# A four-layer graph network on one core: the stages between the edge passes reworked, dense loops four tiles a bank at depth 128

## What is computed

```
layer 0: x = layernorm(x + sum over edges into a node of gathered, weighted rows)
layer 1: two-head attention with 5 edge attributes; the softmax runs over the edges
         of a source node; x = layernorm(x + mean of heads + bias)
layer 2: h = layernorm(x)*g+b; two-head attention (query of the destination node,
         key and value of the source node and 32 edge attributes), softmax over the
         edges into a node; res = x + out@Wp + bp;
         x = layernorm(x + res + gelu(layernorm(res)@W1 + b1)@W2 + b2)
layer 3: spline convolution: each edge weighs 8 matrices by 3 attributes; mean over
         edges, + x@root, batch norm over nodes, ELU, + x, layernorm
```

## Time and profile before

| | us |
|---|---|
| median of three runs (range) | 11246.22 (11240.04 to 11255.09) |
| the profiled execution, time | 11246.92 |
| the profiled execution, span of the trace | 11245.1 |
| VectorE busy | 7124.9 (63%) |
| GpSimd busy | 6918.7 (62%) |
| ScalarE busy | 4592.4 (41%) |
| TensorE busy | 3078.5 (27%) |

### The profile page before, as it was taken

One profiled execution on the slowest core, in us unless ns is written; L12 is line 12 of the kernel. 1 busy time (PEld: TensorE's weight loads), 2 busy tenths in 40 slices (PEclk: granted clock), 3 DMA queues, 4 the chain that ended last, 5 costly groups with the idle time before them and its releaser, 6 DMA issues. The chain is left out here.

```text
span 11245.1 us, 92785 instructions
## 1 busy us (share of the span) xinstructions
PE 3078.5 (27%) x20703; PEld 2546.4 (23%) x20703; DVE 7124.9 (63%) x9873; ACT 4592.4 (41%) x5918; POOL 6918.7 (62%) x6628
## 2 busy tenths in 40 slices
PE   1111366573000000000004566666664720000000
PEld 1111366563000000000003355555553310000000
DVE  6767788886311222118995488888885357777775
ACT  0111255452011111116772377777773234444441
POOL 6777787664577777770002577777773057777774
PEclk9999977776555555555555577777775555555555
DMA  3232322221333332224551344444441067777773
GB/s 98 78 75 89 86 64 68 70 70 51 50 111 107 111 111 103 102 100 184 200 206 43 92 136 130 128 135 129 129 135 52 23 200 235 235 235 235 235 234 90
DMA packets 722526, 1395.98 MB, mean 124 GB/s; under 512 B 409267, under 2 KB 439162, under 8 KB 714834
## 3 DMA queue, kind: packets, MB, share of 16 engines
q0 software_dynamic: 287136, 587.26, 19.4%
q1 hardware_dynamic: 406318, 636.04, 17.1%
q10 hardware_dynamic: 28996, 171.86, 4.1%
HBM read 827.48 MB, written 602.51 MB: 127 GB/s over the span
## 5 line engine op out<-in xcount | busy, mean ns | idle before, releaser
L740 POOL DMA_INDIRECT l_rows<-in_x,l_idx x1568 | 1954.3, 1246 | 669.1 <-issue 490.7
L2180 POOL DMA_INDIRECT l_rows<-table,l_idx x1568 | 1499.5, 956 | 926.9 <-issue 472.6
L1719 POOL DMA_INDIRECT l_rows<-h,l_idx x1568 | 1564.6, 998 | 614.3 <-issue 475.9
L1123 POOL DMA_INDIRECT rows<-l_rows,l_idx x1568 | 1522.6, 971 | 537.0 <-issue 497.0
L1748 PE MATMUL l_made<-l_kv_w,l_rows_t 97*128 97x256 f32 x3136 | 1139.6, 522 | 781.5 <-ACT l_kv L1778 472.4
L2255 ACT ACTIVATE l_lifted<-l_rows,l_up 128x256 f32<-128x256 f32 x1568 | 639.6, 460 | 1041.6 <-DMA l_rows<-table,l_idx 1041.6
L1748 PEld LDWEIGHTS l_made<-l_kv_w,l_rows_t 97*128 97x128 f32 x3136 | 784.2, 267 | 996.4 <-issue 852.5
L1511 PE MATMUL l_wide<-l_diag,l_ones 128*128 128x384 f32 x4 | 3.3, 928 | 3144.9 <-DVEq L1538 3144.9
L1113 DVE TENSOR_TENSOR l_rows<-l_run,l_weights_ps 128x56 f32<-128x56 f32 x56 | 12.0, 215 | 1340.9 <-POOLq L88 1340.7
L1080 ACT COPY l_rows<-l_run 128x1792 f32<-128x1792 f32 x56 | 190.7, 3405 | 1578.5 <-POOLq L88 1569.6
L826 ACT COPY l_out<-l_run 128x1792 f32<-128x1792 f32 x56 | 190.4, 3401 | 1339.5 <-DVE l_run L776 1339.5
(11 more groups left out here) (366 smaller groups left out, 12787.7 us busy)
## 6 DMA issues: line engine op xcount, KB each, us to landing
sums<-l1s_out ACTq DMA_DIRECT2D x56, 1988.0 KB, 6.6
sums<-l_out SPq DMA_DIRECT2D x112, 924.0 KB, 4.5
spread<-zeros SPq DMA_DIRECT2D x28, 3612.0 KB, 12.9
l_spread<-spread SPq DMA_DIRECT2D x112, 903.0 KB
l1s_rows<-rows SPq DMA_DIRECT2D x56, 1008.0 KB, 5.7
spread<-zeros SPq DMA_DIRECT2D x56, 938.0 KB
l_spread<-spread SPq DMA_DIRECT2D x56, 938.0 KB, 4.6
sums<-l_out ACTq DMA_DIRECT2D x56, 896.0 KB, 3.7
```

Of the source, the lines that this page charges most:

```text
L740: pool.indirect_dma_start(rows[:, b, t], None, a["x"], bass.IndirectOffsetOnAxis(ap=idx[:, b, t:t + 1], axis=0)) \
L1123: pool.indirect_dma_start(g["rows1_d"], bass.IndirectOffsetOnAxis(ap=idx[:, b, t:t + 1], axis=0), rows[:, b, t], None).then_inc(sent[b], 16)
L1719: pool.indirect_dma_start(rows[:, c.r, t, 0:C], None, g["h2_d"], bass.IndirectOffsetOnAxis(ap=idx[:, c.r, t:t + 1], axis=0)).then_inc(got[ ...
L2180: pool.indirect_dma_start(rows[:, b, t], None, g["table3_d"], bass.IndirectOffsetOnAxis(ap=idx[:, b, t:t + 1], axis=0)) \
```

## The change

Four kinds of edit, all in the stages between passes.

1. **Halves.** The 49 tiles are worked in two parts (24 and 25). In `collect_sums` and `collect_softmax` each part has its own semaphore for its gathers, so VectorE works on the first while GpSimd issues the second. TensorE's corrections get four banks (six in the softmax, three tiles a bank), and the softmax's small operations are replaced by one product for a bank and one sum for a batch of banks; scaling to the mean moved in as well. `normalise` became a class with parts and the squares on ScalarE; where a dense loop follows a gain and shift, it can start after the first part. The output is stored in parts.
2. **Steps moved.** Layer 1's attention weights are made in the program's first block; its copy of `x` is ScalarE's; loads of the output weights, their bias row and the memsets of the pass's tiles stand beside the table scatters; the memsets of the second pass's tiles stand at the end of the pass before. The head gathers are issued before the last 25 scatters (layer 1) or the last one (layer 2). Layer 2's pass loads no longer wait for the set-up of the tiles, and layer 3's pass loads indices before keys and attributes. The product with `root` runs beside the last gathers (class `RootProduct`).
3. **Dense loops.** Layer 1's end takes two tiles (`PAIRS`) a bank and runs through `Pipeline`; layer 2's query, projection and MLP and layer 3's transpositions take four (`QUADS`). The projection takes both heads in one product with depth 128; elsewhere the operands are `[128, ...]` tiles whose rows from 64 (or 70) on are set to zero once. Layer 3's table has four row buffers and four banks.
4. **The end.** Sums over nodes are matmuls with a tile of ones, 512 columns each, that accumulate; ELU is made of two ScalarE functions and fewer VectorE operations.

```diff
+HALF_TILES = (slice(0, 24), slice(24, NT))
...
-        more = s.ps(f"{name}_more", [P, 2, 8, C])
             def _(pool):
-                for i in range(NT):
-                    pool.indirect_dma_start(total[:, i], None, sums_d,
-                                            bass.IndirectOffsetOnAxis(ap=g["end_idx"]["dst"][:, i:i + 1], axis=0)).then_inc(got, 16)
+                for n, at in enumerate(HALF_TILES):
+                    for i in range(at.start, at.stop):
+                        pool.indirect_dma_start(total[:, i], None, sums_d,
+                                                bass.IndirectOffsetOnAxis(ap=g["end_idx"]["dst"][:, i:i + 1], axis=0)).then_inc(got[n], 16)
...
                 for n, group in enumerate(groups):
-                    if n >= 2:
-                        pe.wait_ge(read, n - 1)
+                    if n >= 4:
+                        pe.wait_ge(read, n - 3)
                     for j, i in enumerate(group):
-                        last = nc.tensor.matmul(more[:, n % 2, j], masks[:, i * P:(i + 1) * P], tail[:], start=True, stop=True)
+                        last = nc.tensor.matmul(more[:, n % 4, j], masks[:, i * P:(i + 1) * P], tail[:], start=True, stop=True)
                     last.then_inc(mult, 1)
...
                 node_mask(v, g, g["cross_key"]["dst"], tiles[:], masks).then_inc(masked, 1)
-                v.wait_ge(got, 16 * NT)
-                v.tensor_tensor(total[:], total[:], g["filled"]["dst"][:].unsqueeze(2).to_broadcast([P, NT, C]), ALU.mult)
-                v.drain()
-                for n, group in enumerate(groups):
-                    v.wait_ge(mult, n + 1)
-                    at = slice(group[0], group[-1] + 1)
-                    v.tensor_tensor(total[:, at], total[:, at], more[:, n % 2, 0:len(group)], ALU.add).then_inc(read, 1)
+                for n, at in enumerate(HALF_TILES):
+                    v.wait_ge(got[n], 16 * (at.stop - at.start))
+                    v.tensor_tensor(total[:, at], total[:, at],
+                                    g["filled"]["dst"][:, at].unsqueeze(2).to_broadcast([P, at.stop - at.start, C]), ALU.mult)
+                    v.drain()
+                    for m, group in enumerate(groups):
+                        if at.start <= group[0] < at.stop:
+                            v.wait_ge(mult, m + 1)
+                            of = slice(group[0], group[-1] + 1)
+                            v.tensor_tensor(total[:, of], total[:, of], more[:, m % 4, 0:len(group)], ALU.add).then_inc(read, 1)
+                    if residual is not None:
+                        v.drain()
+                        v.tensor_tensor(total[:, at], total[:, at], residual[:, at], ALU.add)
     return total
...
-                    turn(0)
-                    for i in range(NT):
-                        if i + 1 < NT:
-                            turn(i + 1)
-                        pe.wait_ge(copied, i + 1)
-                        if i >= 2:
-                            pe.wait_ge(read, i - 1)
-                        for h in range(H):
-                            last = nc.tensor.matmul(made[:, i % 2, 0:C], turned_s[:, i % 2, h], out_w[:, h],
-                                                    start=(h == 0), stop=(h == H - 1))
-                        last.then_inc(made_ready, 1)
...
+                    def make(n, tiles):
+                        for j, i in enumerate(tiles):
+                            for h in range(H):
+                                last = nc.tensor.matmul(made[:, n % 2, j * C:(j + 1) * C], turned_s[:, n % 2, (j * H + h) * P:(j * H + h + 1) * P], out_w[:, h],
+                                                        start=(h == 0), stop=(h == H - 1))
+                        return last
+                    pairs.tensor(pe, [turn, make])
...
-        for step in range(NT + self.stages - 1):
+        for step in range(len(self.groups) + self.stages - 1):
             for k in reversed(range(self.stages)):
                 i = step - k
-                if not 0 <= i < NT:
+                if not 0 <= i < len(self.groups):
                     continue
                 if k:
                     pe.wait_ge(self.brought[k - 1], i + 1)
                 if i >= 2:
                     pe.wait_ge(self.brought[k], i - 1)
-                work[k](i).then_inc(self.made[k], 1)
...
+                    for t in (w1, w2, hid_t, act_t):
+                        v.memset(t[C:P], 0.0)
+                    v.drain().then_inc(zeroed, 1)
...
-                    def turn(i):
-                        for h in range(H):
-                            last = nc.tensor.transpose(ps_a[0:C, i % 2, h * P:(h + 1) * P], summed[:, i, h * V2:h * V2 + C], ident[:])
+                    def turn(n, tiles):
+                        for j, i in enumerate(tiles):
+                            last = nc.tensor.transpose(ps_a[:, n % 2, j * P:(j + 1) * P], mean[:, i], ident[:])
                         return last
-                    def project(i):
-                        for h in range(H):
-                            last = nc.tensor.matmul(ps_c[:, i % 2, 0:C], mean_t[:, i % 2, h], wp[:, h], start=(h == 0), stop=(h == H - 1))
+                    def project(n, tiles):
+                        for j, i in enumerate(tiles):
+                            last = nc.tensor.matmul(ps_c[:, n % 2, j * C:(j + 1) * C], mean_t[:, n % 2, j * P:(j + 1) * P], wp[:], start=True, stop=True)
                         return last
-                    pe.wait_ge(loaded, 16 * len(loads))
-                    pe.wait_ge(scaled, 1)
+                    def turn_hidden(n, tiles):
+                        if tiles[0] == HALF_TILES[1].start:
+                            pe.wait_ge(ready, 2)
+                        for j, i in enumerate(tiles):
+                            last = nc.tensor.transpose(ps_a[0:C, n % 2, j * P:(j + 1) * P], hidden[:, i], ident[:])
+                        return last
+                    def first(n, tiles):
+                        return nc.tensor.matmul(ps_b[0:C, n % 2, 0:len(tiles) * P], w1[:], hid_t[:, n % 2, 0:len(tiles) * P], start=True, stop=True)
+                    def second(n, tiles):
+                        for j, i in enumerate(tiles):
+                            last = nc.tensor.matmul(ps_c[:, n % 2, j * C:(j + 1) * C], act_t[:, n % 2, j * P:(j + 1) * P], w2[:], start=True, stop=True)
+                        return last
+                    pe.wait_ge(loaded, 16 * (H + len(loads) + len(depth)))
                     pipe.tensor(pe, [turn, project])
                     pe.wait_ge(ready, 1)
...
-            spline, root = s.sb("l3_spline", [C, S3 * C]), s.sb("l3_root", [C, C])
-            x_t = s.sb("l3_x_t", [C, 2, P])
...
+            spline = s.sb("l3_spline", [P, S3 * C])
+            x_t = s.sb("l3_x_t", [P, 2, 4 * P])
+            row = s.sb("l3_row", [P, 4, S3 * C])
+            ps_a, ps_b = s.ps("l3_psa", [P, 2, 512]), s.ps("l3_psb", [P, 4, 512])
...
-                    def turn(i):
-                        if i >= 2:
-                            pe.wait_ge(brought, i - 1)
-                        nc.tensor.transpose(ps_a[0:C, i % 2, 0:P], x[:, i], ident[:]).then_inc(made, 1)
+                    def turn(n):
+                        if n >= 2:
+                            pe.wait_ge(brought, n - 1)
+                        for j, i in enumerate(QUADS[n]):
+                            last = nc.tensor.transpose(ps_a[0:C, n % 2, j * P:(j + 1) * P], x[:, i], ident[:])
+                        last.then_inc(made, 1)
                     turn(0)
-                    for i in range(NT):
-                        if i + 1 < NT:
-                            turn(i + 1)
-                        pe.wait_ge(brought, i + 1)
-                        if i >= 2:
-                            pe.wait_ge(copied, i - 1)
-                            pe.wait_ge(read, i - 1)
-                        nc.tensor.matmul(ps_b[:, i % 2], x_t[:, i % 2], spline[:], start=True, stop=True)
-                        nc.tensor.matmul(ps_c[:, i % 2, 0:C], x_t[:, i % 2], root[:], start=True, stop=True).then_inc(tabled, 1)
+                    for n, tiles in enumerate(QUADS):
+                        if n + 1 < len(QUADS):
+                            turn(n + 1)
+                        pe.wait_ge(brought, n + 1)
+                        for j, i in enumerate(tiles):
+                            if i >= 4:
+                                pe.wait_ge(copied, i - 3)
+                            nc.tensor.matmul(ps_b[:, i % 4], x_t[:, n % 2, j * P:(j + 1) * P], spline[:], start=True, stop=True).then_inc(tabled, 1)
                 @block.scalar
...
```

More of the change, by code:

```diff
@@ L892, in collect_sums @@
+def collect_sums(nc, sem, g, outer, name, sums_d, tail, residual=None, root=None):
     s0 = Space(nc, outer)
@@ L1224, in source_order_sums @@
+def source_order_sums(nc, sem, g, tail, head_a, held):
     S, T, F, W = SCORED, T1, F1, H * F1
@@ L1517, in _ @@
```

(18 more changed lines are left out.)

796 lines of the change are left out of this document (459 added, 337 removed).

## The result

| | before | after |
|---|---|---|
| median, us (range) | 11246.67 (11240.04 to 11255.09) | 10843.78 (10838.77 to 10871.85) |
| ratio, 95% interval | | 0.9646 (0.9634 to 0.9659) |
| span of the profiled execution | 11245.1 | 10837.0 |
| VectorE / GpSimd / TensorE busy | 7124.9 / 6918.7 / 3078.5 | 7045.1 / 6893.2 / 2930.1 |

What follows compares the result with a forecast made beforehand. GpSimd's gathers in four passes cost most but stay; the change touches 1380 us between passes, chains of engines waiting for each other. 11247 less 270 at 1.2 GHz and 52 for the clock gave 10925, range 10845 to 11000.

Steps and rivals of the forecast that it cites:

- rival 2: The clock also rises in the MLP, projection and layer 1's dense loop: 24+16+32 us more gain, 10853; chance 0.15.
- Collecting sums: Collecting a layer's sums in halves, half beside the gathers: 15 us gained after layer 0, 13 at the end.
- Layer 1's start, memsets, second pass: Stage to layer 1's first scatters, with sums, earlier scatters and moved memsets: 45 gained; memsets moved from second pass's start: 18.
- Layer 1's dense loop: Layer 1's end: pairs turned behind the last product make TensorE wait for ScalarE's copy, 1.75 us a tile: 28 lost.
- Softmax sums: Ends of layers 1 and 2: half the work moves beside the gathers, gaining 19 us and, with uncovered loads, 9.
- Layer 2's start: Copy and squares gone, scatters at their own pitch, earlier head gather, sync queue not waiting for set-up: 35 us gained.
- table at 1.2 GHz and the clock: Layer 3's table: root product moved beside gathers, 30 us gained; zero rows raise the clock, 1.15 a tile, 44 more.
- MLP: Layer 2's end: quads three stages deep and an early start, 122 us become 81 at clock 0.50: 41 gained.
- rival 4: Slower than before: a gather's price shifts in one pass, as from 956 to 1246 ns, 455 us, 11380; chance 0.02.
- Rival 1: TensorE's clock stays at 0.50 despite zero rows, table at 2.05 us a tile: 10977; chance 0.2.
- rival 3: VectorE's half operations and memsets beside GpSimd cost more than counted, 40 us: 10965; chance 0.12.
- rival 5: Dense loops in quads bring nothing since the additions wait for banks, 60 us: 10985; chance 0.06.

Runs made afterwards that it cites:

- e5: The kernel after, with the sums and softmax sums collected over all 49 tiles in one part after all gathers, not in halves: 10878.58 us.
- e4: The kernel after, with the five large memsets put back at the start of layer 1's pass and of its second, source-order pass: 10880.96 us.
- e7: e3 with layer 1's dense-loop products made over their 70 rows, without the zero rows: 10809.40 us.
- e3: The kernel after, with two-stage pipelines (layer 1's dense loop, queries, projection, root product) turning the next bank ahead of this bank's product: 10783.10 us.
- e9: e3 with layer 2's end weights loaded beside the softmax gathers and layer 2's first norm waiting for loads only at the gain: 10768.64 us.
- e1: The kernel after, with zero rows left out of the query, MLP and layer 3 table products (64 rows instead of 128): 10919.56 us.
- e2: The kernel before, with layer 3's table loop operands extended to 128 rows, the upper 64 zero: 11190.43 us.
- e6: The kernel before, with an unused tile of 1200 bytes a partition and three unused semaphores allocated ahead of everything: 11246.67 us.
- e10: The kernel before, unchanged, profiled again: 11246.67 us.

## Why the prediction was nearly right, point by point

The forecast was 10925. The measured 10843.78 lies 81 us below it, at the edge of the range and nearest to rival 2's 10853. It is not there by rival 2's mechanism: of the three loops that rival 2 names, the clock rose in one, the MLP. Most stages came out within 3 us for the reason given. Four terms were too small, the passes, the MLP, the softmax sums and the table, and as all four erred to one side nothing made up for them.

- **Collecting sums (15 and 13).** Right: from the first gather to the norm 92.2 us before (from 2727.49) and 76.5 after (2723.55 to 2800.07), 15.6; at the end 15.1. e5 says that about half of each is the halves'.
- **Layer 1's start, memsets, second pass (45, 18).** Right: 47.8 and 17.8; the open bound 0 to 18 of the memsets closes at 18 (0.98 us beside them; e4). The sum took off 2 where the text names 3 for VectorE beside the scatters and 1 to 2 for the first block, so by its own words it was 42 to 43.
- **Layer 1's dense loop (-28).** Right to 1 us: 3.49 a pair where 3.5 stood. e7, at depth 70 with a pair turned ahead, shows that the order was the cause: 61 us, where the kernel before took 59.4. What the prediction had not seen is that with the order mended the clock rises too: from the kernel after to e3 the loop gains 51, not 28.
- **Softmax sums (19 and 9).** Too small, 26.1 and 18.7. The step that failed is "behind them stay 25 tiles at 0.70": that pace was VectorE's and TensorE's exchange of before. TensorE's corrections need no gathered data, so with six banks most stand ready, and the 25 tiles cost 9 us in joined products and sums (5954.33 to 5963.4) instead of 17.5. The sum also left out the half product behind the last gather, 3.87. In all 19 us stay where 25 were set. The delay of the gathers was 6 (from 73.3 to 79.2 us for 49) where 8 were set. The uncovered loads of layer 2 were as expected: 7.8 from their first issue to TensorE's first product, and e9 got 5.0 of them back.
- **Layer 2's start (35).** Near, in part by luck: 38 with the norm, and the trace has 42.2. The forecast left the queries at 0.50; in this trace they rose, and e4 and e5, where they did not, would make it about 36. 4.5 of it come back in layer 2's pass, where TensorE's first transposition follows the first gather by 21.9 us instead of 19.1.
- **Projection (61), norm (3), table at 1.2 GHz and the clock (74), indices (9), the end (33).** 61.1, 3.2, 79.9, 10.3, 32.3. A tile of the table took 0.97 instead of 1.15, as transfers reached 273 GB/s and left no wait. e1 and e2 show the table's clock to come from the zero rows: taken out, it stays at 0.50, and put into the kernel before, it rises. By the Trainium skill, "TensorE: Matmul & The Clock Gate", section "Part 1: The HAM clock gate", the clock goes by how busy TensorE has been; e1 and e7, full at 0.50 for 96 and 61 us, say that this is not all.
- **MLP (41).** Too small, 62.3: rival 2 in part. The step that failed is "I leave them at 0.50", said for short products and waits. From 8607 on the clock is 0.98, with 26 of 29 us busy; at 0.50 (e1) the loop takes about what was worked out, and 17 of the 21 us are back. Projection and layer 1's loop stayed down, as forecast.
- **Passes (0).** Wrong by 33 us in layers 1 and 3: a gather there costs 13 and 10 ns less (medians 972 to 959, 957 to 947), where the prediction had "gathers at unchanged means". No step names it but rival 4, in the other direction: "a gather's price is not fixed". It moved by 10 to 13 ns, not by 290.
- Rival 1 (clock stays) fell by e1; rival 3 (VectorE beside GpSimd dearer) fell: e4 and e5 show gains where it had losses; rival 5 fell with the projection's 0.88 a tile.

Between the 408 us of the traces and the 322 of the forecast's terms lie 33 of passes, 21 of the MLP, 17 of softmax sums, 6 of the table, 3 at layer 1's start, 4 of the ordering and layer 0, and 2 of small differences. The end of the ordering and layer 0's pass varies by more than its 4 from profile to profile with the same code there (2726.3 to 2741.5 in before, e2, e6 and e10; 2723.6 to 2745.3 in the kernel after and e1, e3, e4, e5, e7, e9), so the 4 are no gain of the change that these runs could show.

## What to carry to other kernels

Count a stage's waits, not its work, when it stands between passes: estimates by start and end of each step held to 1 or 2 us wherever the order of instructions was read. Where a dense loop on TensorE is full at clock 0.50, try zero rows up to 128 and a bank turned ahead together: in layer 1's loop both brought 51 us, zero rows alone gave nothing at all, and a bank ahead alone gave back only its waits. A product took 421 ns at clock 0.50 with 70 rows and with 128; what the zero rows do cost is their memsets, 2.7 us ahead of the projection in e9. Read the granted clock of a loop in more than one trace before a few us are put down to an edit: the queries' loop went either way with the same code. After a change, compare the price of one unchanged instruction in all passes: a few ns on 1568 of them can outweigh a stage.

## What the runs showed of the hardware that was not expected

- Depth 64 or 70 with TensorE full: clock 0.50 over 110, 96 and 61 us. The same loops with zero rows up to 128: 0.94 to 1.00 in the table, 0.89 over layer 1's loop from its start.
- The same loop with waits can go either way: the queries' ran at 1.00 in the kernel after, 16.7 of 24 us busy, and at 0.50 in e4 and e5, 19.3 and 19.6 of 24 busy. The projection, 34.5 of 43 us busy, stayed at 0.50 in all four traces with that order. What decides it was not tried.
- A memset of VectorE of 3.25 us beside GpSimd's scatters left them at 0.98; a product of two tiles took one to 2.28.
- The price of an indexed transfer is a property of the whole program: 952 to 957 or 944 to 947 ns (layers 2 and 3), 969 to 972 or 958 to 959 (layer 1), and layer 2's table scatters the other way, 966 to 969 or 982 to 984. Why is open.
